# A macaron layer on one core: steps at a token half's end go behind the next gate products, norms take eight slots, and score 0 one slot more

## What is computed

```
x = x + 0.5 * ffn(layernorm(x))
x = x + attn(layernorm(x))
x = x + 0.5 * ffn(layernorm(x))

ffn:  hidden = fwht(silu(x @ W1.T) * (x @ W3.T))      # 2048 wide, Walsh-Hadamard
      out    = hidden @ W2.T
attn: q, k, v = rmsnorm(x) @ quant(qkv_w).T           # 16 heads of 32, chunks of 128 tokens
      scores = q k^T * decay mask;   o = scale * (scores v + decay * q S);   S = decay * S + k^T v
      out = rmsnorm(rmsnorm(o)) @ quant(proj_w).T
```

## Time and profile before

| | |
|---|---|
| median of three runs | 2315.58 us |
| the profiled execution's own time | 2314.23 us |
| its span, first to last instruction | 2312.4 us |
| TensorE busy | 2278.0 us, 99% |
| VectorE busy | 1544.4 us, 67% |
| ScalarE busy | 882.9 us, 38% |
| mean granted TensorE clock | 0.997 of full speed |

### The profile page before, as it was taken

How to read it: one execution, slowest core, us unless ns; L and a number is a source line. 1 busy time by engine, 2 the same in 40 slices (tenths; PEclk the granted TensorE clock), 3 DMA queues, 4 the chain that set the end, 5 groups by cost and what they waited for, 6 DMA issues and landing times. The chain is left out here.

```text
span 2312.4 us, 48747 instructions
## 1 busy us (share of the span) xinstructions
PE 2278.0 (99%) x19551; PEld 1776.8 (77%) x19551; DVE 1544.4 (67%) x3469; ACT 882.9 (38%) x1845; POOL 212.0 (9%) x206
## 2 busy tenths in 40 slices
PE   9999999999999999999999999999999999999998
PEld 5444444678887888888878888788878888888887
DVE  7677456675777667767766677676677767667544
ACT  7646133433343333334333343333334343334222
POOL 0290014200000000000000000000000000000000
PEclk9999999999999999999999999999999999999999
DMA  9866533344444533555255344632546335343322
GB/s 243 226 159 176 158 105 80 124 125 119 130 119 121 145 91 118 136 141 134 79 147 140 93 127 137 152 89 85 167 115 144 98 91 162 97 117 83 110 92 67
DMA packets 351713, 291.56 MB, mean 126 GB/s; under 512 B 253824, under 2 KB 278656, under 8 KB 348672
## 3 DMA queue, kind: packets, MB, share of 16 engines
q1 hardware_dynamic: 351056, 287.66, 46.6%
q10 hardware_dynamic: 432, 0.79, 0.1%
HBM read 173.02 MB, written 59.77 MB: 101 GB/s over the span
## 5 line engine op out<-in xcount | busy, mean ns | idle before, releaser
L1503 DVE SCALAR_TENSOR_TENSOR work<-l_bank,l_scale,work 128x256 f32<-128x256 f32 x416 | 181.7, 478 | 301.2 <-PE l_bank L1887 300.8
L1915 PE MATMUL d_bank<-w2t,work 128*128 128x256 f16 x2496 | 374.8, 273 | 3.2 <-DVE work L1520 2.1
L1887 PE MATMUL g_bank<-work,w1t 128*128 128x256 f16 x2688 | 315.0, 274 | 6.5 <-ACT work L1152 6.5
L1887 PE MATMUL l_bank<-work,w3t 128*128 128x256 f16 x2688 | 311.7, 273 | 0.0
L1152 ACT ACTIVATE work<-g_bank,g_scale 128x256 f32<-128x256 f32 x416 | 174.8, 469 | 308.9 <-PE g_bank L1887 306.0
L1887 PEld LDWEIGHTS g_bank<-work,w1t 128*128 128x128 f16 x2688 | 260.8, 98 | 40.5 <-ACT work L1152 7.1
L1887 PEld LDWEIGHTS l_bank<-work,w3t 128*128 128x128 f16 x2688 | 261.3, 98 | 33.1
L1520 DVE TENSOR_TENSOR work<-work 128x256 f16<-128x256 f32 (+1 forms) x416 | 256.7, 617 | 29.3 <-ACT work L1164 23.7
L1915 PE MATMUL d_bank<-work 128*128 128x256 f16 x1872 | 272.4, 273 | 0.0
L1915 PEld LDWEIGHTS d_bank<-w2t,work 128*128 128x128 f16 x2496 | 240.6, 98 | 40.8 <-DVE work L1520 2.7
L1887 PE MATMUL g_bank<-xt,w1t 128*128 128x256 f16 x2304 | 267.2, 272 | 2.2 <-ACT work L1152 2.2
(11 more groups left out here) (279 smaller groups left out, 2940.7 us busy)
## 6 DMA issues: line engine op xcount, KB each, us to landing
work<-w_dram SPq DMA_DIRECT2D x208, 384.0 KB, 3.3
work<-parts_dram SPq DMA_DIRECT2D x192, 128.0 KB, 3.1
x_dram<-work SPq DMA_DIRECT2D x16, 1024.0 KB, 4.9
parts_dram<-q_parts SPq DMA_DIRECT2D x32, 256.0 KB, 2.1
parts_dram<-k_parts SPq DMA_DIRECT2D x32, 256.0 KB, 2.3
norm_dram<-cent SPq DMA_DIRECT2D x32, 256.0 KB, 2.0
w2t<-in_L_ffn_W_dram SPq DMA_DIRECT2D x31, 256.0 KB, 3.4
xin<-in_L_attn_x_dram SPq DMA_DIRECT2D x7, 1024.0 KB, 7.4
```

Source lines behind the costliest of these rows:

```text
L1503: nc.vector.scalar_tensor_tensor(out=tokens, in0=l_bank[:, HALF * e:HALF * (e + 1)], scalar=l_scale[:, tile:tile + 1], in1=tokens, op0=ALU ...
L1887: ins = nc.tensor.matmul(dst[:, HALF * e:HALF * (e + 1)], wt[:, wp, k, P * tile:P * (tile + 1)], f.x[:, s_half, xp, k, :], start=(k == 0 a ...
L1915: ins = nc.tensor.matmul(bank_m[:, cols], combos[:, q % 2, hp, combo, :], weights[:, wp, :], start=(p == 0 and opens and hp == wp), stop=( ...
```

## The change

- In the pair of a half's end of the layers after the fourth's first pair, the steps of slot 3p + 2 go behind the next pair's `hgate` and `w2stream`, ahead of slot 3p + 3's (`later`). In the fourth layer this holds for its second half.
- `norm_steps` has a wide form over eight slots: prep and split alternate. It is used for the norms whose tiles are turned into place: `qkv` but for batch 0, `o` and `ffn1` but for the last batch. The `ffn2` norm, the `qkv` norm of batch 0 and the last batch's `o` and `ffn1` keep six slots.
- `score` 0 moves from slot at to at + 1, `sclow` 0 from at + 1 to at + 2; `pv` 0 stays at at + 3. The next group's `k` moves from at + 1 to at; the first group's `q` moves a slot later, to one slot ahead of its `k`.
- `ostat` takes four slots instead of two, the `o` norm begins two slots later, the projection four slots later (two in the last batch), the `ffn2` norm two slots later (one in the last batch), and the last `unpark` one slot later.
- SiLU's second tile goes to a buffer of its own, `second_gate`. It waits until the pair before has had its products taken (`hfull_ready`) and no longer for that pair's second low half; VectorE, which writes the product of this tile to the old place, waits for that low half.
- The rows of x1 for the residual come back in two loads of 512 KB, behind the splits of tiles 1 and 3, instead of four of 256 KB.

```diff
--- before.py
+++ after.py
@@ -111,6 +111,7 @@
         plain_area = work[:, offsets["hid"]:offsets["hid"] + sizes["hid"] + sizes["gate"] + sizes["hfull"]]
         n_combos = 2 * COMBOS * P
         combos = plain_area[:, 0:n_combos].bitcast(F16).rearrange("p (b a i t) -> p b a i t", b=2, a=2, i=COMBOS)
+        second_gate = plain_area[:, n_combos:n_combos + HALF]
         hid_f32 = at["hid_f32"].rearrange("p (i t) -> p i t", i=8)
         w2_sums = at["hid_f32"].rearrange("p (i d) -> p i d", i=4)
         streamed = at["streamed"].bitcast(F16).rearrange("p (b a i d) -> p b a i d", b=2, a=2, i=3)
@@ -256,7 +257,7 @@
         hid_stored = [sem("hid_stored0"), sem("hid_stored1")]
         hid_back = [sem(f"hid_back{j}") for j in range(HT)]
         flipped2 = [sem("flipped2_even"), sem("flipped2_odd")]
-        x1_back = [sem(f"x1_back{t}") for t in range(TT)]
+        x1_back = [sem("x1_back0"), sem("x1_back1")]
         k_turned, kd_f32, kd_hi, kd_lo = sem("k_turned"), sem("kd_f32"), sem("kd_hi"), sem("kd_lo")
         sc_hi, sc_lo = sem("sc_hi"), sem("sc_lo")
         o_stats, o_scaled, o_small = sem("o_stats"), sem("o_scaled"), sem("o_small")
@@ -325,11 +326,13 @@
             base = PER * (n - 2)
             which, batch = ORDER[n]
             last = n == 2 * B - 1
-            steps = [("begin", n)]
+            steps, later = [("begin", n)], []
             for s_half in range(2):
                 for p in range(PAIRS):
                     slot = base + (HT + PAIRS) * s_half + 3 * p
-                    steps += [("hgate", (s_half, p)), ("w2stream", PAIRS * s_half + p)] + slots.get(slot, []) + [("hlin", (s_half, p))]
+                    steps += [("hgate", (s_half, p)), ("w2stream", PAIRS * s_half + p)]
+                    steps += later + slots.get(slot, []) + [("hlin", (s_half, p))]
+                    later = []
                     if which == "ffn2" and not last and p == PAIRS - 1:
                         steps += [("back", (batch, s_half))]
                     if n == FAST and s_half == 0 and p == 0:
@@ -341,10 +344,11 @@
                     if p:
                         steps += [("hdown", (s_half, p - 1))] + slots.get(slot + 2, [])
                     elif s_half:
-                        steps += [("hdown", (0, PAIRS - 1)), ("hout", 0), ("resid", 0), ("resid", 1)] + slots.get(slot + 2, [])
+                        steps += [("hdown", (0, PAIRS - 1)), ("hout", 0), ("resid", 0), ("resid", 1)]
+                        later = slots.get(slot + 2, [])
                     elif n > FAST:
                         steps += [("begin", n - 1), ("hdown", (1, PAIRS - 1)), ("hout", 1), ("resid", 2), ("resid", 3), ("begin", n)]
-                        steps += slots.get(slot + 2, [])
+                        later = slots.get(slot + 2, [])
                     else:
                         steps += slots.get(slot + 2, [])
             if last:
@@ -352,18 +356,20 @@
             return steps
 
 
-        def norm_steps(key):
-            return ([[("stat", key)], [("prep", (key, 0))]]
-                    + [[("split", (key, t - 1)), ("prep", (key, t))] for t in range(1, TT)] + [[("split", (key, TT - 1))]])
+        def norm_steps(key, wide=False):
+            prep, split = [[("prep", (key, t))] for t in range(TT)], [[("split", (key, t))] for t in range(TT)]
+            if wide:
+                return [[("stat", key)], prep[0], split[0] + prep[1], split[1], prep[2], split[2], prep[3], split[3]]
+            return [[("stat", key)], prep[0], split[0] + prep[1], split[1] + prep[2], split[2] + prep[3], split[3]]
 
         def attention_slots():
             slots, taken = {}, {}
 
-            def norm(at, key):
+            def norm(at, key, wide=False):
                 if key[0] in ("ffn1", "qkv"):
                     for t in range(TT):
                         add(slots, at - 2 + t // 2, [("rows", (key, t))])
-                for i, steps in enumerate(norm_steps(key)):
+                for i, steps in enumerate(norm_steps(key, wide)):
                     assert at + i not in taken, (key, at + i, taken[at + i])
                     taken[at + i] = key
                     add(slots, at + i, steps)
@@ -372,17 +378,18 @@
                 first = FIRST_NORM + PERIOD * b
                 if 0 < b < B - 1:
                     add(slots, first - 11, [("fetch", b)])
-                norm(first, ("qkv", b))
+                norm(first, ("qkv", b), wide=b > 0)
                 heads = [first + 18 + GROUP_PERIOD * g for g in range(GROUPS)]
                 for g, at in enumerate(heads):
-                    add(slots, at, [("kv", (b, g)), ("score", (b, g, 0)), ("state", (b, g))])
-                    add(slots, at + 1, [("sclow", (b, g, 0)), ("statestore", (b, g)), ("statespread", (b, g))])
+                    add(slots, at, [("kv", (b, g)), ("state", (b, g))])
+                    add(slots, at + 1, [("score", (b, g, 0)), ("statestore", (b, g)), ("statespread", (b, g))])
+                    add(slots, at + 2, [("sclow", (b, g, 0))])
                     for c in range(1, TT):
                         add(slots, at + 2 * c, [("score", (b, g, c))])
                         add(slots, at + 2 * c + 1, [("sclow", (b, g, c)), ("pv", (b, g, c - 1))])
                     add(slots, at + 9, [("pv", (b, g, TT - 1))])
                 for g, at in enumerate(heads):
-                    k_at, q_at = (at - 11, at - 4) if g else (at - 7, at - 9)
+                    k_at, q_at = (at - 12, at - 4) if g else (at - 7, at - 8)
                     add(slots, k_at, [("k", (b, g))])
                     add(slots, k_at + 1, [("klow", (b, g))])
                     add(slots, q_at, [("q", (b, g))])
@@ -393,23 +400,25 @@
                     add(slots, at - 2, [("kdlow", (b, g))])
                 add(slots, heads[0] - 4, [("v", (b, 0)), ("v", (b, 1))])
                 add(slots, heads[0] - 3, [("v", (b, 2)), ("v", (b, 3))])
-                end = heads[-1] + 9
-                add(slots, end + 1, [("projload", b), ("ostat", (b, 0)), ("ostat", (b, 1))])
-                add(slots, end + 2, [("ostat", (b, 2)), ("ostat", (b, 3))])
-                norm(end + 3, ("o", b))
+                end, last = heads[-1] + 9, b == B - 1
+                add(slots, end + 1, [("projload", b)])
                 for t in range(TT):
-                    add(slots, end + 9 + t, [("proj", (b, t))])
-                add(slots, end + 9 + TT, [("keep", b)])
-                out_norm = first + PERIOD + 6 if b < B - 1 else end + 10 + TT
+                    add(slots, end + 1 + t, [("ostat", (b, t))])
+                norm(end + 5, ("o", b), wide=not last)
+                proj = end + (11 if last else 13)
                 for t in range(TT):
-                    add(slots, out_norm - 5 + t if b < B - 1 else end + 10 + t, [("rows", (("ffn2", b), t))])
+                    add(slots, proj + t, [("proj", (b, t))])
+                add(slots, proj + TT, [("keep", b)])
+                out_norm = proj + TT if last else first + PERIOD + 8
+                for t in range(TT):
+                    add(slots, out_norm - TT - 1 + t if not last else proj + 1 + t, [("rows", (("ffn2", b), t))])
                 norm(out_norm, ("ffn2", b))
             add(slots, 4, [("early", 3)])
             for at, n in LATE_STORES.items():
                 add(slots, at, [("store", n)])
             for at, b in ((19, 3), (109, 4), (253, 5), (353, 6), (470, 7)):
-                norm(at, ("ffn1", b))
-            for at, b in ((80, 0), (156, 1), (234, 2), (312, 3), (391, 4), (488, 5), (547, 6), (616, 7)):
+                norm(at, ("ffn1", b), wide=b < B - 1)
+            for at, b in ((80, 0), (156, 1), (234, 2), (312, 3), (391, 4), (488, 5), (547, 6), (617, 7)):
                 for t in range(TT):
                     add(slots, at + t, [("unpark", (b, t))])
             return slots
@@ -885,10 +894,10 @@
                             operand_free(ORDER.index(key))
                         sp.dma_start_transpose(token_tile(target, t).rearrange("p a k t -> p (a k) t"), turned
                                                ).then_inc(flipped[t % 2], 16)
-                    if key[0] == "o" and key[1] < B - 1:
-                        if t == 0:
-                            sp.wait_ge(x1_stored, 16 * (key[1] + 1))
-                        sp.dma_start(x2[:, t, :], x1_dram[key[1], :, t, :]).then_inc(x1_back[t], 16)
+                    if key[0] == "o" and key[1] < B - 1 and t % 2:
+                        two = slice(t - 1, t + 1)
+                        sp.wait_ge(x1_stored, 16 * (key[1] + 1))
+                        sp.dma_start(x2[:, two, :], x1_dram[key[1], :, two, :]).then_inc(x1_back[t // 2], 16)
                 elif step == "unpark":
                     batch, t = arg
                     sp.wait_ge(flipped[t % 2], flips(("ffn2", batch), t))
@@ -1148,8 +1157,11 @@
                         act.wait_ge(w2_sum_lo, 2 * PAIRS)
```

(13 more changed lines are left out.)

## The result

The changed kernel takes 2324.6 us (median of 4 runs, 2323.4 to 2325.8) against 2315.5 for the kernel before: a ratio of 1.0038, 95% interval 1.0026 to 1.005. The forecast was 2317.0 with a range of 2306 to 2321, and "slower" had a chance of 0.20. The profiled execution took 2323.4 us with a span of 2321.6, 9.2 more than the 2312.4 before.

What follows compares the result with a forecast made beforehand. TensorE, busy 99%, was taken as the bound, so only its waits counted. Terms −6.7 − 5.6 − 0.9 − 0.5 − 2.3 + 0.3 + 17.1 = +1.4 us gave 2317.0 us, range 2306 to 2321.

Steps and rivals of the forecast that it cites:

- The mechanism that sets the sign: After the third layer, p·v 0 waits 0.61 us for the moved `sclow` 0 in 28 groups: 17.1 us slower.
- A: Rival: p·v 0 doesn't wait for `sclow` 0; 2299.9 us, chance 0.12.
- B: Rival: VectorE reaches q in time, half's ends cured altogether; up to 10.5 us more gained, 2306.5 us, chance 0.17.
- C: Rival: VectorE stays late and score 0 waits for k's copy; 2321 to 2323 us if 0.2-0.3 late, chance 0.18.
- D: The prediction's own sum of all terms holds: 2312 to 2321 us, chance 0.53.
- p·v 0 behind `sclow` 0: 28 groups: p·v waits 0.61 us each, +17.1 us, plus 0.3 in batch 6 where the ffn1 norm shares the slot.
- The new wait in batches 2 and 6: Behind the half's end, late VectorE makes k wait for q's low half: 1.7 us in each batch.
- "Both go" in the o norm: Half's end, batches 3 and 7: SiLU's waits and batch 3's projection wait go, 5.6 us gained.
- Score 0's DMA waits: Three scores waiting for the spread of q or k by DMA stop waiting, score 0 being a slot later: 2.3 us gained.
- q and k of the first group: Batches 1 and 5: k's 2.96 us wait for q's low half becomes 2.7; 0.5 us gained for both.
- `ostat`, the second buffer, and the loads of x1: Batch 4's `ostat` spread over four slots gains 0.9 us; SiLU's own buffer and fewer x1 loads change nothing.
- "later": Half's ends of batches 2 and 6: SiLU ahead of the norm's copy removes its waits and low clocks, 10.1 us.

Runs made afterwards that it cites:

- e1: Changed kernel with score 0, its low half and k back in their old slots; 2316.8 us, 1.0004 of the kernel before.
- e2: Kernel before with only score 0, sclow 0 and k moved to their new slots; 2333.2 us (1.0077).
- e3: Changed kernel with sclow 0 in the slot of score 0, directly behind it and ahead of the l products; 2306.1 us (0.9959).
- e7: e3 with SiLU's second tile in the pair's own buffer again; 2304.7 us (0.9956).
- e8: e3 with the qkv, o and ffn1 norms over six slots again, in the new first slots; 2306.9 us (0.9964).
- e6: e3 with q of a layer's first group and its low half first in their slot; 2302.7 us (0.9945).
- e12: Kernel before with only q and k of a layer's first group, and their low halves, first in their slots; 2309.2 us (0.9977).
- e5: Kernel before with `later` alone: steps at a half's end behind the next gate products; 2314.0 us (0.9996).
- e10: e3 without `later`: steps at a half's end ahead of the next gate products again; 2306.1 us (0.9963).
- e4: Changed kernel with p·v of chunk 0 one slot later, ahead of score 2; 2314.6 us (0.9996).

## Why the prediction was wrong

The mechanism that sets the sign was forecast, and rivals A, B and C all fail: p·v waits 28 times, the half's ends are not cured, and line 1987, the score, waits for k's copy 0.5 us in all. C named "slower", and its 2321 to 2323 us come nearest to the time, but by another wait than the one that came: that would have been luck. What happened is D with its terms mis-sized by 8 us together, twice the 4 between its forecast and the end of the range: 4.4 us in batches 2 and 6, 2.9 at p·v, 1.6 in the o norm and 1.3 at score 0 too little, and 2.0 too much at q and k.

1. **p·v 0 behind `sclow` 0**: +17.4 taken, +20.3 measured. The step "VectorE's next operation is `sclow` 0, which ends at 1305.53, p·v at 1305.58" is right to the tenth for `sclow`. The 0.05 us between its end and p·v is 0.15, with the weights loaded behind the wait, and at the half's ends the cost is 0.81 and not 0.61. e1, e2 and e3 show the term by taking it away, adding it alone, and curing it.
2. **The new wait in batches 2 and 6**: 1.7 taken for each, 3.9 measured, 4.4 us in sum and the largest miss. My chain followed VectorE and looked for one late step, k's. There are four: a low half, SiLU, the turned tile, q's low half. A late VectorE is paid at each engine that next needs it, SyncE's transposes among them. That VectorE's lateness is behind all four is read from the trace; no run took it away.
3. **"Both go" in the o norm**: 5.65 us went, 1.7 came, 0.85 drawn for weights whose load was issued behind a store and took 6.0 us, and 0.52 for SiLU behind the norm's copy. The step counted VectorE's chain alone, and had SyncE's at nothing. Batch 7 is as forecast.
4. **Score 0's DMA waits**: 2.3 taken, 1.0 to 1.3 measured. The longest of the list's three waits (0.9) lies ahead of the fourth layer. But its true worth shows in e1: with wide norms and the old slot it would be 9 us dearer. My sum took each part against the kernel before, and so never saw it.
5. **q and k of the first group**: 0.5 taken, 2.5 measured. The wait fell from 2.96 drawn to 2.30, and three other batches got 0.15 us each. The low clock that I left in batch 5 was absent, 1.7 of the 2.5, and that is chance: it is there in e7 and e8, and not in e2, where these q and k stand as before. The cause I gave was half right: e6 and e12 show that ScalarE's copy of q stood behind the norm's copy, more than the slot.
6. **`ostat`, the second buffer, and the loads of x1**: as forecast, 0.95, 0 and 0. e7 shows the buffer; the loads weren't tried alone.

The prediction gave "later" 10.1 us. Those waits did go in the full kernel, but e5 and e10 show that the cause was wrong: the norms' slots remove them too, and `later` by itself gives no measurable gain (0.9 us, within the interval). The chain that ends in batches 2 and 6 could have told this, had I asked which step stands at the half's end in the new order.

## What to carry to other kernels

When a step moves a slot later, move what follows from it into the idle time before its reader, or count the reader's wait at every place: 0.70 us in 28 places outweighed every wait that the change cured, and putting one low half beside its score turned 9 us of loss into 9 of gain. On an engine that works in order, look at what stands directly ahead in the same slot: q's and k's copies behind a norm's copy cost 6 us in the kernel before, found by reading their start against their producer's end. And price a part with the others in place, once by leaving it out and once alone; two parts that cure one wait are worth it once.

## What the runs showed of the hardware

The same wait may or may not bring the low clock, a granted clock between the two levels. Behind the wait of k in batch 1, both kernels standing 2.30 us, the granted clock of 519 to 523 us is in the kernel after

```profile
519.00:523.00 4.00, 3.87 (x28) 2.71 (x29) 3.25 (x9) 1.60 (x3) 0.00 (x0) 1.00 0.10 33
```

and in e3

```profile
519.00:523.00 4.00, 3.83 (x12) 1.59 (x13) 3.30 (x9) 1.55 (x3) 0.00 (x0) 0.57 0.08 28
```

and the pair is 2.47 us too long in one and 4.14 in the other. Where it was seen the price was 1.4 to 1.7 us: 1.65 and 1.57 before, 1.67 in e1, e3 and e7, 1.53 in e10, 1.37 in e2. The runs of one kernel differ with it: of the kernel before, beside e1 to e4, the runs of 2310.9, 2316.4 and 2320.4 us had mean clocks of 0.998, 0.996 and 0.994, while the four runs of the kernel after lay within 2.3 us at 0.999 to 1.0. A single profiled execution was up to 4.1 us from its median (e1), so a term of 2 to 4 us in one trace should be looked for in a second.
